# A fused two-layer kernel: second norm and feed-forward in one stage, expert weights in quarters

## The chip, the core and the metric

The kernel runs as one program on one core of a Trainium2 chip. Its time is the device time of one execution in microseconds (us); less is better. The core has five engines that run their own instruction streams and wait for each other through semaphores: PE (matrix products, into the accumulation banks "ps"), DVE (vector operations), ACT (activations and scaled copies), POOL (a second vector engine, slower for the same width) and SP (here only a queue that starts DMA transfers). DMA engines move data and also transpose it.

## The reference

Two layers over x of 4 x 2048 rows of 256 numbers. Each layer is a layer norm, an attention s, a feed-forward g, and x + s * silu(g):

```python
xn = _layernorm(x)
s  = L0_attn(xn)       # linear attention, elu(q)+1, 16 heads
g  = _silu(L0_ffn(xn)) # 16 experts, top 2 by row, and a shared expert
x  = x + s * g
xn = _layernorm(x)
s  = L1_attn(xn)       # retention with decay by head, group norm
g  = _silu(L1_ffn(xn))
return x + s * g
```

The change is mostly about `L1_ffn`. Its two products take operands that are rounded to a 4-bit grid in blocks of 16 numbers, each block scaled by its largest magnitude over 6:

```python
scale = max(max|xb| / 6, 1e-12)
q = grid(|xb / scale|) * sign(xb) * scale  # grid 0 .5 1 1.5 2 3 4 6
gate, y = fp4(x) @ fp4(w_gate).T, fp4(x) @ fp4(w_up).T   # 256 -> 704
g = fp4(silu(gate) * y) @ fp4(w_down).T                  # 704 -> 256
```

## The kernel before

The 8192 rows are 64 tiles of 128 rows. The kernel is a row of stages with a barrier between two; inside a stage each engine walks over the tiles in a software pipeline. `pipeline(eng, count, stages, slots)` is written once per engine with a list of (skew, function): at step c the engine calls, in the order of the list, each function for tile c - skew. So the list is the order of the engine's queue, and an instruction that waits holds up all behind it. The first depth + slots (+ a remainder) steps and the last ones are written out, the rest is a loop with `slots` steps in its body; `unrolled` writes out all.

The stages that matter, with their times in the profiled execution: `phase_dense` (116 to 389 us), `phase_norm_fp4`, named normB (945 to 1097), `phase_ffn` (1097 to 1483), `phase_retention` (1483 to 1838), `phase_output` (1839 to 1909).

normB takes 16 groups of 4 tiles. SP loads a group of x (512 KB, four slots), DVE takes the statistics (`bn_stats`, `bn_aggr`), POOL the reciprocal root, ACT normalises into `xn` and copies the upper part to f16, POOL subtracts for the lower part, and SP turns both (`xT_all`). The rounding is in `Quant`, 1024 wide: on DVE `dve_amax` (L412), `dve_step` (L418), `dve_reciprocal` (L423), `dve_scale` (L432), `dve_round` (L445), `dve_grid` (L451) and `dve_value` (L459), on ACT `act_magic` (L440) and `act_hi` (L464), on POOL `low` (L469). The rounded rows are turned into `xq_T`. PE has nothing to do in this stage.

`phase_ffn` takes one tile a step. PE makes gate and up in two halves of 352 columns (`project(0)`, `project(1)`, 12 products each, lines L197), each in a gate bank and an up bank of its own, and, five tiles later, `down` (L632, 17 products). ACT takes silu of each gate half (`sigmoid`, L647), DVE multiplies it with the up half (`swish`, L674), and the 704-wide result goes through the same `Quant`. SP turns it (`ffn_hT`, four slots), `down` uses it from two banks in turn, and ACT's `output` (L657) writes silu over the tile's place in `xq_T`. PE's `project(k)` waits for `swish(k)` of the tile before, since it writes into the same banks. The weights of the last two stages (`w_pack1`) are loaded and split in f16 parts at the stage's start.

`phase_dense` makes first-layer keys, values, and the shared expert. Meanwhile SP loads one expert's weights every fourth tile (763 columns), ACT makes their upper part (`expert_hi`, L1193), DVE the lower (L1245). `kv_product` (L1131) sums keys x values in one bank over four tiles, then DVE adds that to `kv_sum` (`add_sums`, L1239) and PE waits for it. `phase_retention` is a pipeline with three steps in its loop; DVE's masked product (L2143) comes once a tile. `phase_output` ends with DVE's L2307 and L2311 in groups of four tiles, after POOL's lower parts (L2341).

## Time and profile before

| | |
|---|---|
| median of 3 runs | 1910.14 us (1910.09 to 1916.22) |
| profiled execution | 1911.08 us, its span 1909.3 us |
| mean granted TensorE clock | 0.892 |
| PE busy | 1383.9 us, 72% |
| DVE busy | 1482.7 us, 78% |
| ACT busy | 1183.7 us, 62% |
| POOL busy | 1055.7 us, 55% |
| second norm, PE busy | 0 of 153 us |
| feed-forward, PE busy | 366 of 386 us |

The shares are means over stages with different limits, so no single one tells what bounds the kernel. The stages follow one another with barriers between them, and a stage's length has to be read from the engine that is full in it, or from the loop of waits that closes over it. A granted clock of 1.00 in a stretch is 2.4 GHz.

### The profile page before, as it was taken

The page shows a single profiled execution, that of the slowest core. Times are in us where ns is not written, and L with a number is a line of the kernel's source. Part 1 is how long each engine was busy: PE and PEld are TensorE (multiplying, and loading weights), DVE is VectorE, ACT ScalarE, POOL GpSimd, SP SyncE. Part 2 cuts the span into 40 slices and gives each one's busy share as a digit, 9 for nine tenths or more (in the row PEclk, how much of TensorE's full clock was granted, in tenths as well). Part 3 has the DMA queues.
Part 4 walks back from the last instruction along what each step waited for, and adds up shares of the span by engine and source line. Part 5 has one row for each costly group of instructions (what it writes and reads, how often), then busy time and mean ns, then how long its engine had stood idle before and what let it go on. Part 6 is the DMA issues. An engine that isn't in the chain of part 4 may idle for free. (4 is left out here: it accounts for less than half of the span.)

```text
span 1909.3 us, 63051 instructions
## 1 busy us (share of the span) xinstructions
PE 1383.9 (72%) x21895; PEld 956.3 (50%) x21896; DVE 1482.7 (78%) x3716; ACT 1183.7 (62%) x2966; POOL 1055.7 (55%) x1056
## 2 busy tenths in 40 slices
PE   3469999968998355455300089999998779999957
PEld 3425555546555244344200056666666456666646
DVE  7876777756665599888499789999998568888849
ACT  7637777846666488888266444444444557777746
POOL 6657777733333787775156512222222467777747
PEclk9999999989999677777655599999999999999959
DMA  8636666689997576766469723223223112222229
GB/s 257 194 121 174 188 181 187 179 163 207 213 218 193 164 188 181 189 166 156 134 143 196 146 68 64 65 60 68 60 60 68 41 42 54 51 55 50 55 72 294
DMA packets 487154, 256.17 MB, mean 134 GB/s; under 512 B 357309, under 2 KB 474624, under 8 KB 486528
## 3 DMA queue, kind: packets, MB, share of 16 engines
q1 hardware_dynamic: 474466, 219.10, 46.1%
q0 software_dynamic: 12576, 35.67, 6.4%
q8 instruction: 59, 0.97, 0.2%
q14 instruction: 53, 0.43, 0.1%
HBM read 79.52 MB, written 73.44 MB: 80 GB/s over the span
## 5 line engine op out<-in xcount | busy, mean ns | idle before, releaser
L197 PE MATMUL ps<-all_late,l_xq_T 128*128 128x352 f16 x1536 | 244.4, 317 | 170.1 <-DVEq L185 159.5
L197 PEld LDWEIGHTS ps<-all_late,l_xq_T 128*128 (+1 forms) x1536 | 147.3, 99 | 262.6 <-DVEq L185 160.0
L469 POOL TENSOR_TENSOR ffn_h<-ffn_fq_val,ffn_h 128x704 f16<-128x704 f32 x64 | 97.4, 1522 | 286.9 <-ACT ffn_h L464 286.9
L197 PE MATMUL ps<-l0moe_W,all_xT_all 128*128 128x16 f16 (+2 forms) x1152 | 190.6, 312 | 40.0 <-ACT all_xT_all L828 22.3
L647 ACT ACTIVATE ffn_th<-ps 128x352 f32<-128x352 f32 x128 | 59.3, 463 | 178.3 <-PE ps L197 178.3
L1362 POOL TENSOR_TENSOR all_late<-experts_se,all_mhalf 128x4 f32<-128x4 f32 (+1 forms) x77 | 76.6, 995 | 158.8 <-DVE experts_se L1471 149.6
L2215 POOL TENSOR_TENSOR all_late<-ret_pm,all_late 128x512 f16<-128x512 f32 x128 | 145.5, 1157 | 19.4 <-ACT all_late L2121 19.4
L197 PEld LDWEIGHTS ps<-l0moe_W,all_xT_all 128*128 (+1 forms) x1152 | 83.9, 100 | 122.0 <-ACT all_xT_all L828 26.0
L632 PE MATMUL ps<-all_late,ffn_hT 128*128 128x256 f16 x1088 | 131.7, 276 | 6.0 <-ACT l_xq_T L657 5.4
L197 PE MATMUL ps<-moe_E,experts_gT 128*128 x864 | 117.5, 276 | 16.9 <-DMA experts_gT<-slots_dram 12.4
L1627 PE MATMUL ps<-l_kvm,both_q 128*128 128x136 f16 x384 | 38.9, 272 | 118.4 <-DVE both_o L1800 118.4
L632 PEld LDWEIGHTS ps<-all_late,ffn_hT 128*128 128x128 f16 x1088 | 107.0, 99 | 25.7 <-issue 4.9
L2143 DVE TENSOR_TENSOR ret_pm<-ps,tables_causal 128x1024 f32<-128x1024 f32 x64 | 78.4, 1225 | 44.9 <-PE ps L1988 32.9
L197 PE MATMUL ps<-l1b_W,all_xT_all 128*128 128x512 f16 x384 | 97.1, 392 | 2.4 <-DVEq L1911 2.4
L197 PEld LDWEIGHTS ps<-moe_E,experts_gT 128*128 128x128 f16 x864 | 71.8, 98 | 50.6 <-issue 32.8
L1627 PEld LDWEIGHTS ps<-l_kvm,both_q 128*128 128x128 f16 x384 | 33.2, 121 | 124.2 <-issue 123.9
L2103 ACT ACTIVATE all_late<-ps,tables_parity 128x512 f16<-128x512 f16 x128 | 81.3, 694 | 16.7 <-PE ps L2003 16.7
L1435 ACT ACTIVATE all_late<-ps 128x510 f32<-128x510 f32 x72 | 42.9, 595 | 71.8 <-PE ps L1411 49.5
L2084 ACT ACTIVATE all_xT_all<-ps 128x256 f32 (+1 forms) x64 | 24.5, 383 | 97.1 <-PE ps L2048 97.1
L197 PE MATMUL ps<-moe_E,experts_hT 128*128 x432 | 69.7, 275 | 18.8 <-issue 5.7
L1662 POOL DMA_INDIRECT both_y<-rows_dram,moe_pos_lo x64 | 72.9, 1139 | 18.1 <-issue 16.7
L1615 PE MATMUL ps<-all_xT_all,l_Wq 128*128 128x256 f16 x384 | 67.4, 345 | 20.9 <-DVE both_qp L1781 14.4
(295 smaller groups left out, 4511.1 us busy)
## 6 DMA issues: line engine op xcount, KB each, us to landing
rows_dram<-all_late SPq DMA_DIRECT2D x72, 256.0 KB, 2.5
ret_v<-ret_vpad SPq DMA_DIRECT2D x256, 64.0 KB, 2.0
front_xin<-x SPq DMA_DIRECT2D x16, 512.0 KB, 4.5
x_dram<-front_x SPq DMA_DIRECT2D x16, 512.0 KB, 5.4
all_late<-x_dram SPq DMA_DIRECT2D x64, 128.0 KB, 2.1
z_dram<-all_late SPq DMA_DIRECT2D x64, 128.0 KB
both_zin<-z_dram SPq DMA_DIRECT2D x16, 512.0 KB, 4.8
both_xin<-x SPq DMA_DIRECT2D x16, 512.0 KB, 4.3
```

The costliest lines, as they stand in the source:

```text
L197: mm = pe.matmul(out, lhs[a], rhs[b], start=first and n == 0, stop=last and n == 2, skip_group_check=True)
L469: eng.tensor_tensor(lo, self.shaped(t, hi), hi, ALU.subtract).then_inc(self.lo, 1)
L632: ins = pe.matmul(down_ps[t.slot], hT[:, t.slot4, c % both], DN[:, c], start=c == 0, stop=c == both + FFC - 1, skip_group_check=True)
L647: act.activation(th[:, t.slot, k], gate[k], ACT.Silu, scale=1 / WS).then_inc(s_th[k], 1)
L1362: pool.tensor_tensor(rows[:, n % 4, which, :, 0], se[:, u, which], power[:, which], ALU.pow).then_inc(s_time, 1)
L1435: act.activation(os[t.slot4][:, :, 1:D], op[t.slot], ACT.Copy, scale=1 / WS).then_inc(s_oc, 1)
L1615: ins = pe.matmul(qps[t.slot][:, j], w[a], x[:, :, b * C + c], start=c == 0 and n == 0 and j == 0, stop=c == C - 1 and n == 2, skip_group_ ...
L1627: ins = pe.matmul(nps[:, k, c], q16[:, t.slot, a, c, k * P:(k + 1) * P], kv[b], start=c == 0 and n == 0, stop=n == 2, skip_group_check=True)
L1662: pool.indirect_dma_start(dst[:, slot, k], None, rows_dram, at).then_inc(arrived[slot], 16)
L2103: ins = act.activation(kx16[:, t.slot4].rearrange("p a c s e j -> p (a c s) e j")[:, :, e], src, ACT.Copy, scale=parity[:, e:e + 1])
L2143: dve.tensor_tensor(pm[:, t.slot4], sps, causal[:].unsqueeze(1).to_broadcast([P, 4, RC]), ALU.mult).then_inc(s_p, 1)
L2215: ins = pool.tensor_tensor(p16[:, u, 1, r], pm[:, u, r], p16[:, u, 0, r], ALU.subtract)
```

## The change

**Second norm and feed-forward in one stage.** `phase_norm_ffn` replaces both. Norm and rounding of x go by pairs of tiles (512 wide) on the even or odd steps, eleven steps (K) ahead of the projections of the same tiles. x is loaded by pairs (256 KB) in two slots, and a load waits until ACT has normalised the pair two before. x and xn lie in the memory of the later weights W1, so `w_pack1` is loaded and split at the stage's end.

**Products on POOL.** For the hidden values, `QuantApart` writes the grid to SBUF (`dve_grid`), and the product with the step is POOL's (`pool_value`). The first half of the swish product is POOL's too; it needs the up half in SBUF, so ACT copies it (`up_copy`, 352 wide). `down` has one bank instead of two, its skew is 8 instead of 5, and the turned hidden values have two slots instead of four.

```diff
+def pipeline(eng, count, stages, slots=LAG, head=None):
...
+    start = depth + (slots if head is None else head) + (count - depth) % slots
...
+class QuantApart(Quant):
...
+    def dve_scale(self, dve, t, src):
+        u = t.slot
+        dve.wait_ge(self.rs, done(t))
+        dve.wait_ge(self.q, self.work_free(t))
+        dve.scalar_tensor_tensor(self.b3(self.work[u]), self.b3(src), 1 - 2.0 ** -22,
+                                 self.wide(self.rstep[u]), ALU.mult, ALU.mult).then_inc(self.v, 1)
+    def act_magic(self, act, t):
+        u = t.slot
+        act.wait_ge(self.v, done(t))
+        act.wait_ge(self.xq, free(t))
+        act.activation(self.big[:, u], self.work[u], ACT.Abs, scale=self.MAGIC).then_inc(self.mg, 1)
+    def dve_grid(self, dve, t):
+        u = t.slot
+        dve.wait_ge(self.up, done(t))
+        dve.scalar_tensor_tensor(self.big[:, u], self.big[:, u], self.LEAST, self.work[u],
+                                 ALU.max, ALU.subtract).then_inc(self.q, 1)
...
+    def pool_value(self, pool, t):
+        u = t.slot
+        pool.wait_ge(self.q, done(t))
+        pool.wait_ge(self.hi, free(t))
+        pool.wait_ge(self.lo, free(t))
+        pool.tensor_tensor(self.b3(self.val[:, u]), self.b3(self.big[:, u]), self.wide(self.step[:, u, 0:self.blocks]),
+                           ALU.mult).then_inc(self.xq, 1)
```

```diff
+def phase_norm_ffn(nc, ps, x_dram, mhalf, xT_all, xq_T, GU, DN, W1, apart, loads, jobs):
...
+        h16 = ph.sb("h16", [P, LAG, 2 * FF], F16)
...
+        down_ps = ps[:, 6, 0:D]
+        at = [FF + u * 64 for u in range(2 * LAG)]
+        fq = QuantApart(ph, "fq", FF, 1.0, work=[spare[:, 0:FF]],
+                        rstep=[spare[:, at[u]:at[u] + FF // BLK] for u in range(LAG)])
+        nq = Quant(ph, "nq", U * D, 1.0, work=[ps[:, 7, :]],
+                   rstep=[spare[:, at[LAG + u]:at[LAG + u] + U * D // BLK] for u in range(LAG)])
...
+            def load(p):
+                if p.n >= LAG:
+                    sp.wait_ge(s_xn, p.n - LAG + LAG + 1)
+                sp.dma_start(xin[:, p.slot], x_pairs[p.n]).then_inc(s_xin[p.slot], 16)
...
+            def turn_h(t):
                 sp.wait_ge(fq.lo, done(t))
-                through(sp, s_pass)
...
+                sp.wait_ge(s_down, free(t))
+                sp.dma_start_transpose(hT[:, t.slot], h16[:, t.slot]).then_inc(s_hT[t.slot], 16)
+            unrolled(TILES, [(0, even(load)), (6, even(turn_x)), (9, even(turn_q)), (K + 6, turn_h)], 4)
+            sp.wait_ge(s_wlo, 1)
+            sp.dma_start(stage, jobs[1][0]).then_inc(s_stage[1], 16)
```

```diff
-                    pe.wait_ge(s_h[k], prev(t))
+                    if k == 0:
+                        if t.slot4 % 2 == 0:
+                            pe.wait_ge(s_qturn[t.slot4 // 2], landed(pair_of(t)))
+                        pe.wait_ge(s_th[0], prev(t))
+                        pe.wait_ge(s_upc, prev(t))
+                    else:
+                        pe.wait_ge(s_h[1], prev(t))
...
+                pe.wait_ge(s_g, prev(t))
...
-            pipeline(pe, TILES, [(5, down), (0, project(0)), (0, project(1))], 4)
+            pipeline(pe, TILES, [(8, down), (0, project(0)), (0, project(1))], 4)
...
+                act.wait_ge(nq.v, free(p))
...
+            def up_copy(t):
+                act.wait_ge(s_up[0], done(t))
+                act.activation(up0[:, t.slot], upp[0], ACT.Copy, scale=1 / WS).then_inc(s_upc, 1)
...
-            pipeline(act, TILES, [(0, sigmoid(0)),
-                                  (6, output),
-                                  (0, sigmoid(1)),
-                                  (2, hidden_hi),
-                                  (1, lambda t: fq.act_magic(act, t))], 4)
+                act.activation(out, down_ps, ACT.Silu, scale=1 / WS).then_inc(s_g, 1)
...
+            pipeline(act, TILES, [(K, sigmoid(0)), (K, up_copy), (6, even(lambda p: nq.act_magic(act, p))),
+                                  (K + 5, hidden_hi), (K, sigmoid(1)), (K + 8, output), (3, even(normalise)),
+                                  (4, even(upper)), (7, even(quantised_hi)), (K + 8, weights_hi),
+                                  (K + 2, lambda t: fq.act_magic(act, t))], 4)
```

```diff
+                dve.wait_ge(s_xin[u], landed(Tile(t.n // 2, u, t.n // 4)))
+                dve.bn_stats(stats[:, u, k], xin[:, u, k]).then_inc(s_stats, 1)
...
+                dve.wait_ge(s_th[1], done(t))
+                dve.wait_ge(fq.v, free(t))
+                dve.scalar_tensor_tensor(h[:, u, half:FF], th[:, u, 1], 1 / WS, upp[1],
+                                         ALU.mult, ALU.mult).then_inc(s_h[1], 1)
...
-            pipeline(dve, TILES, [(1, swish(0)),
...
-                                  (2, lambda t: fq.dve_round(dve, t)),
-                                  (1, lambda t: fq.dve_step(dve, t)),
-                                  (2, lambda t: fq.dve_grid(dve, t)),
-                                  (1, lambda t: fq.dve_reciprocal(dve, t)),
-                                  (2, lambda t: fq.dve_value(dve, t)),
-                                  (1, lambda t: fq.dve_scale(dve, t, h[:, t.slot]))])
...
+            pipeline(dve, TILES, [(0, statistics),
+                                  (K + 1, swish),
+                                  (K + 2, maxima),
+                                  (1, even(variance)),
+                                  (K + 3, lambda t: fq.dve_round(dve, t)),
+                                  (K + 2, lambda t: fq.dve_step(dve, t)),
+                                  (5, even(maxima_norm)),
+                                  (6, even(lambda p: nq.dve_round(dve, p))),
+                                  (K + 3, lambda t: fq.dve_grid(dve, t)),
+                                  (K + 2, lambda t: fq.dve_reciprocal(dve, t)),
+                                  (5, even(lambda p: nq.dve_step(dve, p))),
+                                  (6, even(lambda p: nq.dve_grid(dve, p))),
+                                  (5, even(lambda p: nq.dve_reciprocal(dve, p))),
+                                  (5, even(lambda p: nq.dve_scale(dve, p, flat(xn[:, p.slot])))),
+                                  (K + 2, lambda t: fq.dve_scale(dve, t, h[:, t.slot])),
+                                  (6, even(lambda p: nq.dve_value(dve, p))),
+                                  (K + 8, weights_lo)], 4)
...
+                pool.tensor_tensor(h[:, u, 0:half], th[:, u, 0], up0[:, u], ALU.mult).then_inc(s_h[0], 1)
+            pipeline(pool, TILES, [(K + 1, swish),
+                                   (2, even(rsqrt)),
+                                   (K + 4, lambda t: fq.pool_value(pool, t)),
+                                   (5, even(part_lo)),
+                                   (8, even(quantised_lo)),
+                                   (K + 5, lambda t: fq.low(pool, t, h16[:, t.slot, 0:FF], h16[:, t.slot, FF:2 * FF]))], 4)
```

**Dense stage, retention, output.** Expert weights come in quarters (191 columns), one a tile; the key-value sums stay in the bank for a batch of 16 tiles, two banks in turn, and DVE copies them once a batch; PE and DVE are written out. Retention's PE starts its loop three steps earlier. In the output stage `prod` has one buffer.

```diff
+                at = quarter(t.n % 4)
+                sp.dma_start(e_stage[:, t.n % 4, 0:at.stop - at.start], e_dram[t.n // 4][:, at]).then_inc(s_eload[t.n % 4], 16)
             unrolled(TILES, [(7, turn), (0, rows_in), (11, expert_load), (12, store)])
...
+                batch, first = t.n // TB, t.n % TB == 0
+                if first and batch >= 2:
+                    pe.wait_ge(s_kvadd, batch - 1)
...
-                        ins = pe.matmul(sums[:, c, 0:P + 1], keys[x], vals[y], start=c == 0 and n == 0 and t.slot4 == 0,
...
-            pipeline(pe, TILES, [(7, down), (3, kv_product), (0, project)], 4)
+            unrolled(TILES, [(7, down), (3, kv_product), (0, project)], 4)
...
-                if t.slot4 == 0:
-                    act.wait_ge(s_eload, 16 * (t.n // 4) + 16)
...
+                at = quarter(t.slot4)
+                act.wait_ge(s_eload[t.slot4], 16 * (t.n // 4) + 16)
...
+                act.activation(part, e_stage[:, t.slot4, 0:at.stop - at.start], ACT.Copy, scale=WS).then_inc(s_ehi, 1)
+            pipeline(act, TILES, [(8, z_out), (3, hidden_hi), (2, key_hi), (1, nonlinear), (10, expert_hi)], 4)
...
-                dve.tensor_tensor(acc[:, :, 0:P + 1], sums[:, :, 0:P + 1], acc[:, :, 0:P + 1], ALU.add).then_inc(s_kvadd, 1)
+                if t.n % TB == TB - 1:
+                    dve.wait_ge(s_kvs, done(t))
+                    dve.tensor_copy(kv_sum[:, t.n // TB, :, 0:P + 1], sums[t.n // TB % 2][:, :, 0:P + 1]).then_inc(s_kvadd, 1)
...
-                                  (1, elementwise)], 4)
...
+            unrolled(TILES, [(4, add_sums), (3, hidden_lo), (2, key_lo), (1, elementwise), (11, expert_lo)], 4)
...
-            pipeline(pe, TILES, [(4, scores), (3, turn), (0, project), (3, updates), (2, queries), (5, results)], 3)
+            pipeline(pe, TILES, [(4, scores), (3, turn), (0, project), (3, updates), (2, queries), (5, results)], 3, head=0)
...
+                if t.n:
+                    dve.wait_ge(s_sum, t.n)
```

How the order moves: on ACT in the middle of the feed-forward stage, two steps of before (ffn_th is silu of a gate half, l_xq_T the output, ffn_h the upper part, ffn_fq_big the magic number's sum):

```order
L647 ACTIVATE ffn_th<-ps 128x352
L657 ACTIVATE l_xq_T<-ps 128x256
L647 ACTIVATE ffn_th<-ps 128x352
L464 ACTIVATE ffn_h<-ffn_fq_val 128x704
L440 ACTIVATE ffn_fq_big<-ps 128x704
L647 ACTIVATE ffn_th<-ps 128x352
L657 ACTIVATE l_xq_T<-ps 128x256
L647 ACTIVATE ffn_th<-ps 128x352
L464 ACTIVATE ffn_h<-ffn_fq_val 128x704
L440 ACTIVATE ffn_fq_big<-ps 128x704
```

And two steps of after, an even one first (l_apart<-l_W is the pair's upper part, ffn_up the copy of the up half, l_W<-l_W the normalising of a pair, ffn_nq the pair's rounding):

```order
L641 ACTIVATE ffn_th<-ps 128x352
L655 ACTIVATE l_xq_T<-ps 128x256
L631 ACTIVATE l_apart<-l_W 128x2x256
L396 ACTIVATE ffn_fq_big<-ps 128x704
L641 ACTIVATE ffn_th<-ps 128x352
L646 ACTIVATE ffn_up<-ps 128x352
L359 ACTIVATE ffn_h<-ffn_fq_val 128x704
L641 ACTIVATE ffn_th<-ps 128x352
L655 ACTIVATE l_xq_T<-ps 128x256
L624 ACTIVATE l_W<-l_W,ffn_shift,ffn_rstd 128x256 x2
L359 ACTIVATE l_apart<-ffn_nq_val 128x2x256
L396 ACTIVATE ffn_fq_big<-ps 128x704
```

The output now stands behind the second silu of the step instead of ahead of it, and the pair's normalising (x2) behind the output, in every other step.

On DVE, one step of before in the same stage:

```order
L412 TENSOR_REDUCE ffn_fq_amax<-ffn_h 128x44
L445 SCALAR_TENSOR_TENSOR ps<-ffn_fq_big,ps 128x704
L418 TENSOR_SCALAR ffn_fq_step<-ffn_fq_amax 128x45
L451 SCALAR_TENSOR_TENSOR ps<-ffn_fq_big,ps 128x704
L423 RECIPROCAL ps<-ffn_fq_step 128x44
L459 TENSOR_TENSOR ffn_fq_val<-ps,ffn_fq_step 128x704
L432 SCALAR_TENSOR_TENSOR ps<-ffn_h,ps 128x704
L674 SCALAR_TENSOR_TENSOR ffn_h<-ffn_th,ps 128x352 x2
```

And an even step of after (ffn_stats is the norm's statistics of one tile, ffn_nq the pair's rounding):

```order
L676 BN_STATS ffn_stats<-l_W 128x6
L697 SCALAR_TENSOR_TENSOR ffn_h<-ffn_th,ps 128x352
L307 TENSOR_REDUCE ffn_fq_amax<-ffn_h 128x44
L340 SCALAR_TENSOR_TENSOR ps<-ffn_fq_big,ps 128x704
L383 TENSOR_SCALAR ffn_fq_step<-ffn_fq_amax 128x45
L340 SCALAR_TENSOR_TENSOR ps<-ffn_nq_big,ps 128x512
L401 SCALAR_TENSOR_TENSOR ffn_fq_big<-ffn_fq_big,ps 128x704
L318 RECIPROCAL ps<-ffn_fq_step 128x44
L346 SCALAR_TENSOR_TENSOR ps<-ffn_nq_big,ps 128x512
L389 SCALAR_TENSOR_TENSOR ps<-ffn_h,ps 128x704
L354 TENSOR_TENSOR ffn_nq_val<-ps,ffn_nq_step 128x512
```

The statistics, which wait for the load of x, come first in each step, ahead of the one swish half that is left; the value product is gone and three 512-wide operations of the pair are in.

On SP in the middle of the new stage, where before there was one turn of hidden values a tile:

```order
L563 DMA_TRANSPOSE l_xq_T<-l_apart 128x8x128
L576 DMA_TRANSPOSE ffn_hT<-ffn_h 128x11x128
L554 DMA l_W<-x_dram 128x2x256
L558 DMA_TRANSPOSE all_xT_all<-l_apart 128x8x128
L576 DMA_TRANSPOSE ffn_hT<-ffn_h 128x11x128
L563 DMA_TRANSPOSE l_xq_T<-l_apart 128x8x128
L576 DMA_TRANSPOSE ffn_hT<-ffn_h 128x11x128
```

The pair's load (l_W<-x_dram), its two turns, and the turns of hidden values (ffn_hT) share this queue.

## Rows read from the trace of the kernel before

**Rows 1.** The windows by stage: stretch, length, busy time of each engine, PE clock, DMA share.

```profile
944.00:1097.00 153.00, 0.00 (x0) 0.00 (x0) 132.02 (x273) 80.35 (x112) 85.96 (x64) 0.50 0.76 165
1200.00:1460.00 260.00, 255.98 (x1874) 179.96 (x1873) 250.49 (x411) 124.14 (x228) 70.03 (x46) 1.00 0.28 62
1483.00:1556.00 73.00, 54.29 (x1985) 36.02 (x1984) 44.72 (x111) 38.45 (x97) 38.96 (x50) 0.91 0.17 41
650.00:900.00 250.00, 137.30 (x1100) 113.07 (x1101) 220.67 (x546) 206.92 (x503) 192.20 (x155) 0.75 0.68 174
```

**Rows 2.** The line that scales the hidden values: count, min/median/max ns, first and last start.

```profile
L432 DVE SCALAR_TENSOR_TENSOR ps<-ffn_h,ps x64: 895/897/897, 1106.6 to 1468.1; 128x704 f32<-128x704 f32 x64
```

**Rows 3.** The groups of 1103 to 1477 us: busy us, mean ns, idle before, releaser.

```profile
L674 DVE SCALAR_TENSOR_TENSOR ffn_h<-ffn_th,ps 128x352 f32<-128x352 f32 x128 | 60.8, 514 | 6.9 <-ACT ffn_th L647 6.8
L432 DVE SCALAR_TENSOR_TENSOR ps<-ffn_h,ps 128x704 f32<-128x704 f32 x64 | 57.4, 897 | 6.6
L423 DVE RECIPROCAL ps<-ffn_fq_step 128x44 f32<-128x44 f32 x64 | 27.4, 428 | 0.0
L418 DVE TENSOR_SCALAR ffn_fq_step<-ffn_fq_amax 128x45 f32<-128x45 f32 x64 | 11.6, 181 | 0.0
L647 ACT ACTIVATE ffn_th<-ps 128x352 f32<-128x352 f32 x128 | 59.3, 463 | 178.3 <-PE ps L197 178.3
L469 POOL TENSOR_TENSOR ffn_h<-ffn_fq_val,ffn_h 128x704 f16<-128x704 f32 x64 | 97.4, 1522 | 286.9 <-ACT ffn_h L464 286.9
```

**Rows 4.** The groups of 940 to 1103 us (the norm).

```profile
L320 DVE BATCH_NORM_STATS2 normB_stats<-normB_xin 128x6 f32<-128x256 f32 x64 | 22.4, 411 | 2.7 <-DMA normB_xin<-x_dram 2.7
L451 DVE SCALAR_TENSOR_TENSOR ps<-normB_fq_big,ps 128x1024 f32<-128x1024 bf16 x16 | 19.6, 1227 | 0.0
L423 DVE RECIPROCAL ps<-normB_fq_step 128x64 f32<-128x64 f32 x16 | 8.8, 552 | 0.0
L357 ACT ACTIVATE normB_xn<-normB_xin,normB_shift,normB_rstd 128x256 f32<-128x256 f32 x64 | 33.2, 588 | 68.2 <-POOL normB_shift L303 68.2
```

**Rows 5.** The timeline in the feed-forward stage: start, length, instruction, idle before.

```profile
1304.43 3.78 PE L197 MATMUL ps<-all_late,l_xq_T 128*128 128x352 f16 x24
...
1464.03 0.38 ACT L657 ACTIVATE l_xq_T<-ps 128x256 f32<-128x256 f32 x1
1464.55 2.02 PE L632 MATMUL ps<-all_late,ffn_hT 128*128 128x256 f16 x17 [0.73 <-ACT l_xq_T L657]
```

**Rows 6.** The DMA issues: count, KB each, median us from issue to landing.

```profile
all_late<-x_dram SPq DMA_DIRECT2D x64, 128.0 KB, 2.1
normB_xin<-x_dram SPq DMA_DIRECT2D x16, 512.0 KB, 4.4
```

**Rows 7.** Waits of 116 to 389 us: us, times, longest.

```profile
PE ps L1131 <- DVE l0moe_kv_sum L1239: 9.1, 12, 2.8
```

**Rows 8.** PE's timeline in the dense stage, and ACT's at its end.

```profile
144.30 2.75 PE L197 MATMUL ps<-l0moe_W,all_xT_all 128*128 128x512 f16 x12
148.22 2.75 PE L197 MATMUL ps<-l0moe_W,all_xT_all 128*128 128x512 f16 x12
...
215.28 2.75 PE L197 MATMUL ps<-l0moe_W,all_xT_all 128*128 128x512 f16 x12
219.20 2.75 PE L197 MATMUL ps<-l0moe_W,all_xT_all 128*128 128x512 f16 x12
...
386.61 0.84 ACT L1193 ACTIVATE moe_E<-dense_e_stage 128x763 f16<-128x763 f32 x1 [1.65 <-DMA dense_e_stage<-e_pack]
```

**Rows 9.** The masked product's line in two windows: count, first and last start.

```profile
L2143 DVE TENSOR_TENSOR ret_pm<-ps,tables_causal x8: 1224/1225/1226, 1501.8 to 1554.9; 128x1024 f32<-128x1024 f32 x8
...
L2143 DVE TENSOR_TENSOR ret_pm<-ps,tables_causal x25: 1223/1225/1226, 1575.5 to 1695.6; 128x1024 f32<-128x1024 f32 x25
```

**Rows 10.** Waits of 1500 to 1556 us (retention).

```profile
PE ps L1988 <- issue: 8.9, 9, 1.9
```

**Rows 11.** The output stage's low parts on POOL: min/median/max ns.

```profile
L2341 POOL TENSOR_TENSOR out_y<-all_late,out_y x16: 2122/3112/3128, 1850.5 to 1896.3; 128x1024 f16<-128x1024 f32 x16
```

368 lines of the change are left out of this document (163 added, 205 removed).

## The prediction

> **What bounds the kernel now.** I read the windows by stage first, since the page's shares mix stages. In the norm PE does nothing for 153 us, while DVE is busy for 132; in the steady feed-forward PE is busy for 255.98 of 260 us and DVE for 250.49, at a granted clock of 1.00 [rows 1]. So one stage is DVE's alone and the other is nearly full on two engines; the change can give back only idle time of PE in the norm, if DVE has room for the norm. Next, the scaling line gives the pitch of a tile: (1468.1 - 1106.6) / 63 = 5.74 us [rows 2]. A tile then costs PE 5.61 us (255.98 / 260 of 5.7) and DVE 5.49. The norm runs from 944.9 (first load) to 1097.5 and the feed-forward to 1482.8: 537.9 us that the new stage replaces.
>
> **DVE in the new stage.** Per tile before: two swish halves 2 x 0.514, five 704-wide operations (scale, maxima, round, grid, value) at 0.89 by the scale's row, reciprocal 0.428, step 0.181: 6.09 us by sum, 5.49 by the clock, as neighbours overlap (factor 0.90) [rows 1, 3]. The change takes away one swish half and the value product: 6.09 - 0.51 - 0.88 = 4.69, 9.38 a pair. It adds the norm of a pair. A wide operation costs 0.897 at 704 and 1.227 at 1024, so by the line through both 0.70 at 512; five of them 3.46 (maxima and value a little less); two statistics at 0.411; the reciprocal between 0.428 at 44 blocks and 0.552 at 64, by the line 0.35 at 32; five small ones near 0.17 [rows 3, 4]. That is 5.5. Pair: 14.9 by sum, times 0.90 = 13.4 us, 6.7 a tile.
>
> **POOL and ACT.** POOL takes 1.522 us at 704 and, undisturbed, 2.122 at 1024, so 0.86 at 352 and 1.16 at 512 [rows 3, 11]. A pair is 2 x (0.86 + 1.52 + 1.52) + 2 x 1.16 and two small ones for the root, some 11: 5.6 a tile, below DVE. The value product reads a bf16 grid, which no row shows on POOL; between 1.52 and, as in the slow rows of the output stage, 1.52 x 3.112 / 2.122 = 2.2. I take 1.52, because in its own stage the 704-wide operation kept that value beside the same DVE operations; the far end is a rival. ACT gains a 352-wide copy and the pair's work, some 9.6 us a pair, and bounds nothing by its sum.
>
> **The rings.** With sums of 6.7, 5.6 and 5.6, the waits decide. Ring one: `down` now has a single bank, and its output stands behind the second silu on ACT. `down` (tile t) waits for the output of the tile before, which waits for that silu, which waits for the step's last projection. So nothing of PE covers silu 0.46 and output 0.38: 5.61 + 0.1 + 0.46 + 0.38 + 0.14 = 6.65 us a tile. The 0.14 is from the end of output to the next product, 1464.41 to 1464.55; the 0.1 is my value for the way from PE to ACT [rows 3, 5].
>
> Ring two closes over the load, once a pair. A pair's load waits for the normalising of the pair two before, which ACT does behind silu and output in the odd step. The statistics, which wait for the load to land, stand first in DVE's next step, ahead of the swish half for which PE's projection waits. A 256 KB load is between 2.1 (128 KB) and 4.4 us (512 KB) [rows 6]; by the line 2.87. From the odd step's silu: silu 0.44, output 0.36, normalising 2 x 0.588 less overlap 1.08, load 2.87, statistics 0.33, swish 0.51, hand-over 0.15, half of the 24 products (3.78 us [rows 5]) with its run-out 2.01: 7.75. The even half is ring one again, 6.65 with rounding 6.70. 14.45 a pair, 7.23 a tile. It is longer than DVE's 6.7, so DVE waits for the load in each pair. Bounds: with a load of 2.1, 6.84 a tile, with 4.4 it is 7.99. I take 7.23.
>
> **The stage.** Fill until the first projection: 2.9 us for the load and 5.5 pairs at DVE's 4.8 (5.5 x 0.9 less what waits on nothing) = 29. Steps 12 to 18 have no `down`: 7 x 6.6 = 46. Then 45 steps with loads, 45 x 7.23 = 325. Then 11 steps without norm in ring one, 11 x 6.65 = 73. Tail: eight `down` at about 2.5 each through the single bank (1.85 and the output's way), 20, the last weights' split and the barrier 4.5: 24.5. Sum 497.5 against 537.9: **-40.4**. Bounds by the load alone: -57 to -6. One barrier fewer is in this sum.
>
> **Dense stage.** PE waits for the key-value sum 12 times, 9.1 us [rows 7]. The stage is full on PE otherwise (3.92 us a tile both in the written-out head, 144.30 to 148.22, and in the loop, 215.28 to 219.20 [rows 8]), so these 9.1 go. At its end the last output stood behind a weights' part that had waited for a DMA by 1.65 us, until 387.4 [rows 8]; quarters have four slots and land earlier, some 2 us more. ACT and DVE get more instructions for the same columns, in stages where neither is full. **-11**; below it 0 if the waits only move, above it -13.
>
> **Retention.** The masked product comes every (1554.9 - 1501.8) / 7 = 7.6 us in the written-out head and the loop's first pass, and every (1695.6 - 1575.5) / 24 = 5.0 in the loop; and PE idles there on "issue" for 8.9 us in 1500 to 1556 [rows 9, 10]. With three written-out steps fewer, three tiles go at 5.0 instead: 3 x 2.6 = **-7.8**; between 0, if the first pass of the loop costs that much wherever it stands, and -12. The trace says that written-out steps of PE are dearer than the loop. The Trainium skill ("Runtime: NRT & Kernel Launch", section "Instruction fetch mechanics") says that fetching a straight stream is mostly hidden, that taken branches break the prefetch, and that kernels prefer full unrolling where possible. By that rule this edit would bring 0 or lose, and the dense stage's unrolling would be the gain. The trace does not agree in retention, and shows no difference either way in the dense stage.
>
> **Output.** DVE now waits for its own previous sum before L2307. It does L2307 and L2311 in that order anyway, and POOL bounds that stage (most of its operations take 3.1 us [rows 11]): +0.2.
>
> **Sum.** 1911.1 (the profiled execution, 1.0 above the median) - 40.4 - 11 - 7.8 + 0.2 = 1852.1. The forecast is 1852 us, 3.1% less; with the terms' nearer ends 1838 to 1868.
>
> **The rivals.**
> - Load ring does not close. If ACT is far enough ahead of DVE in the odd step, the load is hidden, and DVE with 6.7 bounds the stage: 45 x 0.53 = 24 us less, 1828, from 1815 to 1836. For it speaks that a 128 KB load lands in 2.1 [rows 6]; against it, that ACT's normalising stands behind a silu that waits for PE in the same step.
> - POOL is slowed by DVE. In the output stage POOL's operation goes from 2.122 to a median of 3.112 while DVE adds two operands from SBUF [rows 11]. With a factor 1.47 a pair costs POOL 16.2 us, 8.1 a tile: 52 x 0.87 = 45 more, 1897, from 1875 to 1910. Against it: no wide DVE operation of the new stage has both operands in SBUF, as the old ones had none beside L469, which kept 1.522 [rows 3]. The Trainium skill ("GPSIMD Engine Reference", section "8. Key points") says that POOL shares its SBUF interfaces with DVE and collides with DVE instructions in a two-port mode or with two SBUF inputs. By that rule the output stage slows and this one does not; the trace agrees in both.
> - The smaller parts give nothing. The dense waits were covered by ACT and DVE (DVE waits for ACT there too), and the retention's first loop pass keeps its price: 18.8 us back, 1871.
> - PE's clock falls; this one ends on the other side. PE loses its full share (5.6 of 7.23, 77%) with gaps of 0.9 to 1.3 us in each step. Where it was busy for 137 of 250 us the granted clock was 0.75, and where it was busy for 54 of 73 us, 0.91 [rows 1]. At half speed (1.2 GHz) the 7.7 us of products on ring two double. At a mean of 0.91 (18% of the time at half) a pair costs 1.4 more: +36 us, 1888. At 0.75, 3.85 more: 52 x 1.9 = +100, 1952. The stage has 556.5 us before the whole is no gain; less fill, tail and the last steps that is 8.27 a tile, a mean clock of 0.865. Below this the kernel is slower. For it: the gaps are new. Against it: the gaps are short and evenly spread, and 0.75 was seen at a busy share of 55%.
>
> **How the numbers follow.** Forecast 0.48 (1838 to 1868). Load hidden 0.18. POOL slowed 0.11. Smaller parts nothing 0.08. Clock 0.10, half of it below the deciding 0.865. The remaining 0.05 is spread, mostly upwards. The range for 8 in 10 reaches down over most of the load-hidden case and up over the smaller parts, the milder clock and the lower half of POOL's: 1818 to 1892. About 0.5% (10 us) is what a measurement tells from no change. Faster by more needs less than 1900.6: all of the forecast, the hidden load and the smaller parts, most of POOL and half of the clock: 0.90. Within 0.5%: 0.04. Slower: 0.06, the deep clock and one more in a hundred.
>
> **What would show it.** In the profile after: the scaling line's pitch near 7.2 us with a pair pattern, and DVE's statistics waiting for the load of x by 1 to 2 us a pair (if not, the load is hidden, 6.7). PE idle before `down`, ended by ACT's output, about 1 us a tile. POOL's value product at 1.5 us. The granted clock at 1.00. No PE wait for the key-value sum beyond two, the dense stage 11 us shorter; in retention seven slow masked products instead of ten. It would be wrong if the stage is not between 480 and 530 us long, or if an engine that I left out, SP with its turns and loads in one queue above all, holds the pair.

## The result and the profile after

The changed kernel takes 1917.14 us (median of 11 runs) against 1910.34 us in 11 runs of the kernel before: a ratio of 1.003, with a 95% interval of 1.0017 to 1.0043. Ten of the 11 lie between 1914.55 and 1921.14 us; the eleventh took 2066.71 us at a mean granted clock of 0.724 and is left out of the ratio. That is 0.3% slower, within what I had called no change; forecast was 1852, and the range ended at 1892. The profiled execution takes 1917.14 us, its span 1915.3 (1909.3 before).

First the stages. The dense stage ended at 379.4 instead of 392.1 us. The stage that replaces norm and feed-forward runs from its first load at 933.99 to retention's first product at 1492.1 us: 558.1 us, where the two took 537.9 and I forecast 497.5. So 60.6 of the 65 us that the forecast missed by are in this stage, and what is long in it is DVE's pitch, the time from one tile to the next. The scaling line of the hidden values, as in [rows 2] (count, min/median/max ns, first and last start, of the whole stage and of 1100 to 1296 us):

```profile
L389 DVE SCALAR_TENSOR_TENSOR ps<-ffn_h,ps x64: 874/888/896, 974.2 to 1468.3; 128x704 f32<-128x704 f32 x64
...
L389 DVE SCALAR_TENSOR_TENSOR ps<-ffn_h,ps x24: 874/882/890, 1105.4 to 1294.0; 128x704 f32<-128x704 f32 x24
```

(1294.0 - 1105.4) / 23 is 8.20 us a tile, where I had 7.23, and DVE is full in it (length, then busy us of PE, PEld, DVE, ACT, POOL, and the clock, as in [rows 1]):

```profile
1100.00:1400.00 300.00, 211.60 (x1504) 141.00 (x1503) 275.07 (x490) 150.97 (x311) 193.30 (x182) 1.00 0.45 91
```

DVE is busy for 275 of 300 us, so the profile books 7.5 us of work a tile to it, where I had 6.7. PE is busy for 211.6 at a clock of 1.00. The groups of the stage that answer to [rows 3, 4] (busy us, mean ns, idle before and who ended it):

```profile
L389 DVE SCALAR_TENSOR_TENSOR ps<-ffn_h,ps 128x704 f32<-128x704 f32 x64 | 56.6, 884 | 0.3
L697 DVE SCALAR_TENSOR_TENSOR ffn_h<-ffn_th,ps 128x352 f32<-128x352 f32 x64 | 32.2, 503 | 5.1 <-ACT ffn_th L641 4.5
L307 DVE TENSOR_REDUCE ffn_fq_amax<-ffn_h 128x44 f32<-128x704 f32 x64 | 56.1, 876 | 0.0
L383 DVE TENSOR_SCALAR ffn_fq_step<-ffn_fq_amax 128x45 f32<-128x45 f32 x64 | 55.2, 863 | 32.6 <-POOL ffn_fq_val L409 32.6
L313 DVE TENSOR_SCALAR ffn_nq_step<-ffn_nq_amax 128x33 f32<-128x33 f32 x32 | 5.4, 169 | 0.1
L686 DVE TENSOR_SCALAR ffn_away<-ffn_mv 128x2 f32<-128x2 f32 x32 | 25.3, 790 | 3.0
L687 DVE TENSOR_SCALAR ffn_ve<-ffn_mv 128x2 f32<-128x2 f32 x32 | 9.1, 284 | 0.0
L676 DVE BATCH_NORM_STATS2 ffn_stats<-l_W 128x6 f32<-128x256 f32 x64 | 26.3, 415 | 8.9 <-DMA l_W<-x_dram 8.9
L409 POOL TENSOR_TENSOR ffn_fq_val<-ffn_fq_big,ffn_fq_step 128x704 f32<-128x704 bf16 x64 | 89.5, 1399 | 2.3 <-DVE ffn_fq_big L401 1.8 <-POOL ffn_h L364 0.2
L754 POOL TENSOR_TENSOR ffn_h<-ffn_th,ffn_up 128x352 f32<-128x352 f32 x64 | 59.6, 931 | 164.7 <-DVE ps L389 164.7
L364 POOL TENSOR_TENSOR ffn_h<-ffn_fq_val,ffn_h 128x704 f16<-128x704 f32 x64 | 97.5, 1523 | 15.5 <-ACT ffn_h L359 15.5
```

The wide operations cost what they had cost. But L383, the step of 45 numbers, has gone from 181 to 863 ns, and L686, the sign change of two numbers, takes 790, where before a four-wide one took some 170. Their own line shows the spread:

```profile
L383 DVE TENSOR_SCALAR ffn_fq_step<-ffn_fq_amax x64: 175/1048/1479, 971.9 to 1465.7; 128x45 f32<-128x45 f32 x64
```

175 ns at best, 1479 at worst. What they wait for shows in the timeline (start, length, engine, line; idle before the instruction in brackets):

```profile
1241.25 1.16 POOL L364 TENSOR_TENSOR l_apart<-ffn_nq_val,l_apart 128x512 f16<-128x512 f32 x1
1241.40 1.05 DVE L383 TENSOR_SCALAR ffn_fq_step<-ffn_fq_amax 128x45 f32<-128x45 f32 x1 [1.13 <-POOL ffn_fq_val L409]
...
1247.93 1.15 POOL L743 TENSOR_TENSOR l_apart<-l_W,l_apart 128x512 f16<-128x512 f32 x1
1247.95 1.15 DVE L686 TENSOR_SCALAR ffn_away<-ffn_mv 128x2 f32<-128x2 f32 x1
1249.02 0.16 DVE L687 TENSOR_SCALAR ffn_ve<-ffn_mv 128x2 f32<-128x2 f32 x1
```

At 1241.40 the step starts and lasts until 1242.45; POOL's subtraction ends at 1242.41. At 1247.95 L686 starts and lasts until 1249.10; POOL's ends at 1249.08. The next one, L687, meets POOL between two operations and takes 0.16. So it looks as if a tiny DVE operation is held until POOL's running one is done. All 64 steps agree with that: 57 begin while a POOL operation runs, and each of them ends 0.04 to 0.05 us after it; the seven that begin with POOL idle take 0.18 to 0.19. The rounding of the pair has a step of the same kind, L313, 33 wide. It stays at 169 ns, and 28 of its 32 begin while POOL is idle. In sum 64 x (0.863 - 0.181) = 43.6 us for L383, 32 x 0.62 = 19.8 for L686 and 3.6 for L687: 67 us of busy time that I had not counted. Beside it the step waits for POOL's value product of two tiles before (waits of the whole stage: us, times, longest):

```profile
PE ps L213 <- DVE ffn_h L697: 93.3, 57, 3.8
PE ps L608 <- ACT l_xq_T L655: 57.5, 62, 3.5
DVE ffn_fq_step L383 <- POOL ffn_fq_val L409: 32.6, 33, 1.3
DVE ffn_stats L676 <- DMA l_W<-x_dram: 8.9, 5, 3.5
```

The load's ring, which I had as the bound, costs DVE 8.9 us in all, since DVE comes too late to meet it.

### The profile page after: what moved, and what is told of

Same layout as the page of the kernel before. It is cut to its first block and busy times, and to the rows that moved or that the text cites. A ratio compares the mean times of both kernels' runs of the same rounds, so it can differ in the third digit from the quotient of the medians.

```text
span 1915.3 us, 63179 instructions
## 1 busy us (share of the span) xinstructions
PE 1390.9 (73%) x21895; PEld 953.8 (50%) x21896; DVE 1473.2 (77%) x3767; ACT 1199.0 (63%) x3126; POOL 1205.7 (63%) x1248
## 5 line engine op out<-in xcount | busy, mean ns | idle before, releaser
L213 PE MATMUL ps<-all_late,l_xq_T 128*128 128x352 f16 x1536 | 256.9, 320 | 121.7 <-DVE ffn_h L697 93.3
L396 ACT ACTIVATE ffn_fq_big<-ps 128x704 bf16<-128x704 f32 x64 | 48.5, 757 | 191.3 <-DVE ps L389 191.3
L754 POOL TENSOR_TENSOR ffn_h<-ffn_th,ffn_up 128x352 f32<-128x352 f32 x64 | 59.6, 931 | 164.7 <-DVE ps L389 164.7
L608 PEld LDWEIGHTS ps<-all_late,ffn_hT 128*128 128x128 f16 x1088 | 102.7, 99 | 92.8 <-ACT l_xq_T L655 61.8
L213 PEld LDWEIGHTS ps<-l0moe_W,all_xT_all 128*128 128x128 f16 x1152 | 84.0, 100 | 120.5 <-ACT all_xT_all L889 26.0
L2202 DVE TENSOR_TENSOR ret_pm<-ps,l_apart 128x1024 f32<-128x1024 f32 x64 | 78.4, 1224 | 39.9 <-PE ps L2047 38.5
L213 PE MATMUL ps<-l_W,all_xT_all 128*128 128x512 f16 x384 | 96.7, 389 | 5.9 <-DVEq L1970 4.8
L2162 ACT ACTIVATE all_late<-ps,l_apart 128x512 f16<-128x512 f16 x128 | 81.5, 695 | 18.1 <-PE ps L2062 18.1
L409 POOL TENSOR_TENSOR ffn_fq_val<-ffn_fq_big,ffn_fq_step 128x704 f32<-128x704 bf16 x64 | 89.5, 1399 | 2.3 <-DVE ffn_fq_big L401 1.8
L1494 ACT ACTIVATE all_late<-ps 128x510 f32<-128x510 f32 x72 | 42.9, 596 | 69.0 <-PE ps L1470 36.5
```

Of the source, the lines that this page charges most:

```text
L213: mm = pe.matmul(out, lhs[a], rhs[b], start=first and n == 0, stop=last and n == 2, skip_group_check=True)
L409: pool.tensor_tensor(self.b3(self.val[:, u]), self.b3(self.big[:, u]), self.wide(self.step[:, u, 0:self.blocks]), ALU.mult).then_inc(self. ...
L608: ins = pe.matmul(down_ps, hT[:, t.slot, c % both], DN[:, c], start=c == 0, stop=c == both + FFC - 1, skip_group_check=True)
L754: pool.tensor_tensor(h[:, u, 0:half], th[:, u, 0], up0[:, u], ALU.mult).then_inc(s_h[0], 1)
L2162: ins = act.activation(kx16[:, t.slot4].rearrange("p a c s e j -> p (a c s) e j")[:, :, e], src, ACT.Copy, scale=parity[:, e:e + 1])
L2202: dve.tensor_tensor(pm[:, t.slot4], sps, causal[:].unsqueeze(1).to_broadcast([P, 4, RC]), ALU.mult).then_inc(s_p, 1)
```

## The experiments

The theory (A): DVE's small tensor_scalar has SBUF on both sides and needs an access to SBUF that it shares with POOL; it can't start its work while a POOL operation runs. The rival (B): nothing is held, the long operations are waits for POOL's value or for a result, booked as busy time. Ratios are against the kernel before, run beside them on the same chip. The chips differ a little (the kernel before took 1915.92 us beside some of these runs and 1911.85 beside others), so runs are compared by their ratios or by the length of the stage, which is that of the profiled execution.

**One operand from a bank.** The step takes its floor of 1e-12 from an accumulation bank, so the operation is another kind with the same work. The pair's step (L313) is changed in the same way.

```diff
-        dve.tensor_scalar(self.step[:, u], self.amax[:, u], 1 / 6, 1e-12, ALU.mult, ALU.max).then_inc(self.st, 1)
+        dve.scalar_tensor_tensor(self.step[:, u], self.amax[:, u], 1 / 6, self.floor, ALU.mult, ALU.max).then_inc(self.st, 1)
```

> The changed kernel, but DVE's step operation takes its second operand from an accumulation bank (scalar_tensor_tensor with a constant 1e-12 there) in place of the immediate; same width, place and result. Theory A (the small tensor_scalar with SBUF on both sides is held until the POOL operation that runs ends): the step's mean falls from 863 ns to about 200, the stage from 558 us to about 525, the time to about 1884 us; the norm's away operation stays at about 790 ns. Rival B (the 863 ns are a wait for POOL's value product, or for a result, that is booked as busy time): the mean stays over 700 ns and the time at 1917.

Measured: 1879.51 us, ratio 0.980 (0.978 to 0.982), stage 520.0 us. Of the profile's groups, the step and L686, still of the old kind (here L696):

```profile
L388 DVE SCALAR_TENSOR_TENSOR ffn_fq_step<-ffn_fq_amax,ps 128x45 f32<-128x45 f32 x64 | 12.6, 197 | 32.7 <-POOL ffn_fq_val L414 32.7
L696 DVE TENSOR_SCALAR ffn_away<-ffn_mv 128x2 f32<-128x2 f32 x32 | 25.3, 789 | 3.0
```

The step is at 197 ns and the sign change, which was left alone, at 789. The pair's step, which had not been slow, went from 169 to 174 ns, so it has no part in the gain. B is wrong: the wait for POOL's value is still there, as idle time of 32.7 us beside the operation, as it was before the edit.

**The variance's two operations as well.** They also move behind `dve_round` in DVE's list.

```diff
-                dve.tensor_scalar(away[:, p.slot], mv[:, p.slot, :, 0], -1.0, None, ALU.mult)
-                dve.tensor_scalar(ve[:, p.slot], mv[:, p.slot, :, 1], EPS_LN, None, ALU.add).then_inc(s_ve, 1)
+                dve.scalar_tensor_tensor(away[:, p.slot], mv[:, p.slot, :, 0], -1.0, spare[:, 1008:1010], ALU.mult, ALU.add)
+                dve.scalar_tensor_tensor(ve[:, p.slot], mv[:, p.slot, :, 1], 1.0, spare[:, 1010:1012], ALU.mult, ALU.add).then_inc(s_ve, 1)
...
-                                  (1, even(variance)),
                                   (K + 3, lambda t: fq.dve_round(dve, t)),
+                                  (1, even(variance)),
```

> As the run before, and the norm's two small operations away and ve take a second operand from a bank too, and stand behind the round operation. Theory A: away falls from 790 ns to about 180, 32 x 0.6 = 20 us of DVE, the time to about 1866. Rival B: no change from the run before.

Measured: 1864.34 us, ratio 0.973 (0.971 to 0.974). The stage is 496.7 us long. My sum for it was 497.5. The profiled execution was the fastest of the four, though (1857.37 us): by the medians this edit brought 15.2 us, and the 23.3 by which the stage is shorter than in the run before are too many.

```profile
L696 DVE SCALAR_TENSOR_TENSOR ffn_away<-ffn_mv,ps 128x2 f32<-128x2 f32 x32 | 5.0, 156 | 2.9
L686 DVE BATCH_NORM_STATS2 ffn_stats<-l_W 128x6 f32<-128x256 f32 x64 | 26.7, 421 | 24.4 <-DMA l_W<-x_dram 24.4
```

L696 is at 156 ns, and DVE's idle time before the statistics, ended by the load, has risen from 8.9 to 24.4 us: the load's ring comes into sight as DVE gets faster.

**The same by itself.** A stage behind the output, in the changed kernel, in which DVE does six of each of eight kinds, twice over, in one execution; POOL's subtractions begin at 1926.7 us, when the first round has done the 45- and 2-wide kinds, and fill the whole second.

```diff
+                pool.tensor_tensor(pc[:, n % 4], a[:], b[:], ALU.subtract)   # x72, from SBUF, 704 wide
...
+                    dve.tensor_scalar(o[:, part, n, 0, 0:45], x[:], 1 / 6, 1e-12, ALU.mult, ALU.max)
+                    dve.scalar_tensor_tensor(o[:, part, n, 1, 0:45], x[:], 1 / 6, pz[:, 0:45], ALU.mult, ALU.max)
+                    dve.tensor_scalar(o[:, part, n, 2, 0:45], pz[:, 0:45], 1 / 6, 1e-12, ALU.mult, ALU.max)
+                    dve.tensor_scalar(po[:, 48 * n:48 * n + 45], x[:], 1 / 6, 1e-12, ALU.mult, ALU.max)
+                    dve.tensor_tensor(o[:, part, n, 3, 0:45], x[:], y[:], ALU.max)
+                    dve.tensor_scalar(o[:, part, n, 4, 0:2], x[:, 0:4:2], -1.0, None, ALU.mult)
+                    dve.scalar_tensor_tensor(w[:, part, n, 0:352], a[:, 0:352], 1.0, pz[:, 0:352], ALU.mult, ALU.mult)
+                    dve.tensor_reduce(o[:, part, n, 5, 0:44], c[:], AX, ALU.max)   # by 16
```

> The changed kernel with a stage of its own at the end, in which DVE runs eight kinds of operation six times each, first with POOL idle, then beside POOL's back-to-back 704-wide subtractions from SBUF (1.52 us each). Theory A: the tensor_scalar with SBUF at both ends (45 wide and 2 wide) and the tensor_tensor with two SBUF operands take about 0.18 us alone and up to 1.5 us beside POOL; with one operand or the result in a bank, 0.2 in both; the 352-wide product with one bank operand and the 704-wide maxima do not change. Rival B: none of them changes, or all by the same factor.

The groups of that stage (busy us of all 12, mean ns):

```profile
L2421 POOL TENSOR_TENSOR probe_pc<-probe_a,probe_b 128x704 f32<-128x704 f32 x72 | 117.0, 1667 | 17.3 <-DVEq L2432 17.3
L2443 DVE TENSOR_TENSOR probe_o<-probe_x,probe_y 128x45 f32<-128x45 f32 x12 | 10.3, 925 | 0.0
L2435 DVE TENSOR_SCALAR probe_o<-probe_x 128x45 f32<-128x45 f32 x12 | 9.9, 894 | 0.0
L2445 DVE TENSOR_SCALAR probe_o<-probe_x 128x2 f32<-128x2 f32 x12 | 5.5, 534 | 0.0
L2449 DVE TENSOR_REDUCE probe_o<-probe_c 128x44 f32<-128x704 f32 x12 | 9.7, 882 | 0.0
L2447 DVE SCALAR_TENSOR_TENSOR probe_w<-probe_a,ps 128x352 f32<-128x352 f32 x12 | 5.3, 515 | 0.0
L2439 DVE TENSOR_SCALAR probe_o<-ps 128x45 f32<-128x45 f32 x12 | 1.5, 193 | 0.0
L2437 DVE SCALAR_TENSOR_TENSOR probe_o<-probe_x,ps 128x45 f32<-128x45 f32 x12 | 1.5, 192 | 0.0
L2441 DVE TENSOR_SCALAR ps<-probe_x 128x45 f32<-128x45 f32 x12 | 1.5, 195 | 0.0
```

and DVE's timeline, first two kinds before POOL begins, then the second round, six of a kind in a row:

```profile
1922.79 0.65 DVE L2435 TENSOR_SCALAR probe_o<-probe_x 128x45 f32<-128x45 f32 x6
1925.32 0.78 DVE L2443 TENSOR_TENSOR probe_o<-probe_x,probe_y 128x45 f32<-128x45 f32 x6
...
1933.77 9.23 DVE L2435 TENSOR_SCALAR probe_o<-probe_x 128x45 f32<-128x45 f32 x6
1942.92 0.74 DVE L2437 SCALAR_TENSOR_TENSOR probe_o<-probe_x,ps 128x45 f32<-128x45 f32 x6
1943.59 0.75 DVE L2439 TENSOR_SCALAR probe_o<-ps 128x45 f32<-128x45 f32 x6
1944.26 0.72 DVE L2441 TENSOR_SCALAR ps<-probe_x 128x45 f32<-128x45 f32 x6
1944.90 9.49 DVE L2443 TENSOR_TENSOR probe_o<-probe_x,probe_y 128x45 f32<-128x45 f32 x6
1954.32 4.98 DVE L2445 TENSOR_SCALAR probe_o<-probe_x 128x2 f32<-128x2 f32 x6
```

A was right in each kind. Six tensor_scalars with SBUF at both ends take 0.65 us alone and 9.23 beside POOL, about one for each POOL operation (1.67 us); with the operand or the result in a bank it is 0.72 to 0.75 for six. Two SBUF operands (L2443) go from 0.78 for six to 9.49. The 704-wide maxima from SBUF to SBUF take 882 ns beside POOL, and took 0.89 us in the kernel before: width and place alone don't decide, the kind does. The two tensor_scalars with a bank at one end (L2439, L2441) are of the slow kind and stay fast, so the first edit's gain comes from the bank and not from the other operation. POOL's 72 operations all take 1660 to 1673 ns and begin 1.62 to 1.63 us apart, with DVE at work or not: the short DVE operations cost POOL nothing, and only DVE pays.

**The wait for POOL's value.** Four slots for the step values.

```diff
-        dve.wait_ge(self.xq, free(t))
-        dve.scalar_tensor_tensor(self.step[:, u], ...)
+        dve.scalar_tensor_tensor(self.step4[:, t.slot4], ...)
```

> As the run before, and the step values have four slots, so that DVE's step operation does not wait for POOL's value product two tiles before. If that wait (32.6 us of DVE idle in the changed kernel) is on the path: another 10 to 30 us less, about 1845 us. If it is only where DVE happens to wait for POOL, the wait moves to the round operation and the time stays within 5 us.

Measured: 1857.91 us, ratio 0.969 (0.966 to 0.971), and a stage of 495.1 instead of 496.7. The time fell by 6.4 us by the medians. That is less than the 10 to 30 of a wait on the path; the second expectation, 5 at most, holds nearly, but DVE's idle time moved to the load (36.5 us) and not to the round operation:

```profile
L690 DVE BATCH_NORM_STATS2 ffn_stats<-l_W 128x6 f32<-128x256 f32 x64 | 26.7, 422 | 36.5 <-DMA l_W<-x_dram 36.5
```

and its waits of 1050 to 1350 us (us, times, longest):

```profile
PE ps L618 <- ACT l_xq_T L665: 35.9, 43, 0.9
DVE ffn_stats L690 <- DMA l_W<-x_dram: 21.2, 20, 2.0
```

These are the two rings of the prediction, and (1296.2 - 1099.7) / 28 = 7.02 us a tile is close to its 7.23. Whether they bind, the next two tell, each made alone on top of the four slots.

**Ring one: ACT's output first in its step.**

```diff
-            pipeline(act, TILES, [(K, sigmoid(0)), (K, up_copy), ..., (K, sigmoid(1)), (K + 8, output), (3, even(normalise)),
+            pipeline(act, TILES, [(K + 8, output), (K, sigmoid(0)), (K, up_copy), ..., (K, sigmoid(1)), (3, even(normalise)),
```

> The kernel with four step slots (1858 us), and ACT's output stands first in its step, ahead of the first silu, so the single bank of the down product is read before PE has finished the step's projections. Its tile pitch is 7.02 us in 1100 to 1296 us. If ring one is on the path (PE waits for the output 43 times, 35.9 us in 1050 to 1350): those waits go, the pitch falls towards DVE's 6.4 to 6.6, the time by about 18 to about 1840. If the load's ring alone sets the pair (DVE then waits longer for the load): the time falls by 5 or less.

Measured: 1830.40 us, ratio 0.958 (0.956 to 0.959), stage 472.0 us.

**Ring two: DVE's statistics and variance late.**

```diff
-            pipeline(dve, TILES, [(0, statistics),
+            pipeline(dve, TILES, [
...
-                                  (1, even(variance)),
...
+                                  (0, statistics),
+                                  (1, even(variance)),
                                   (K + 2, lambda t: fq.dve_scale(dve, t, h[:, t.slot])),
```

> The kernel with four step slots, and DVE takes the statistics and variance of the norm near the end of its step instead of at its start, so that the load has most of a step to land. If the load's ring is on the path (36.5 us of DVE idle for the load in the whole stage): the idle time goes, the pitch falls to ring one's 6.65, about 17 us less, 1841. If it is only slack of a DVE that waits anyway: no change, and DVE's idle time moves to the swish half.

Measured: 1830.03 us, ratio 0.958 (0.956 to 0.960), stage 472.1 us. Both stages are 23 us shorter than with four slots alone, and the ratio falls from 0.969 to 0.958 (some 22 us), where I expected 17 or 18; both come to the same place. The pitch in 1100 to 1296 us, of the one and of the other:

```profile
L397 DVE SCALAR_TENSOR_TENSOR ps<-ffn_h,ps x29: 878/882/889, 1104.6 to 1292.5; 128x704 f32<-128x704 f32 x29
```

```profile
L397 DVE SCALAR_TENSOR_TENSOR ps<-ffn_h,ps x29: 876/892/894, 1105.4 to 1292.2; 128x704 f32<-128x704 f32 x29
```

187.9 / 28 and 186.8 / 28: 6.71 and 6.67 us a tile, which is DVE's own sum of the prediction, 6.7. With four slots alone the scaling line begins by turns 7.38 and some 6.65 us after the one before. With the output first it is 7.38 and some 6.05: the load still holds one half of the pair (DVE waits 20.6 us for it in the stage, 36.5 before the edit), and DVE makes up for it in the other. So it takes both rings, one in each half, to exceed DVE's pair. The two runs don't part ring one from DVE cleanly: with the statistics late PE still waits for the output in each tile (24.1 us in 29 times in this window), and 6.67 is ring one's own 6.65 as well.

**All of it, and the output stage.** DVE's product there goes back into the bank, so the addition behind it has one operand from SBUF.

```diff
-                dve.scalar_tensor_tensor(prod[:], ops[t.n % TURNED], 1 / WS, g1_all[...], ALU.mult, ALU.mult).then_inc(s_prod, 1)
+                dve.scalar_tensor_tensor(ops[t.n % TURNED], ops[t.n % TURNED], 1 / WS, g1_all[...], ALU.mult, ALU.mult).then_inc(s_prod, 1)
...
-                dve.tensor_tensor(x1[:, u], prod[:], x1[:, u], ALU.add).then_inc(s_sum, 1)
+                dve.tensor_tensor(x1[:, u], ops[t.n % TURNED], x1[:, u], ALU.add).then_inc(s_sum, 1)
```

> Output first and statistics late together, and in the output stage DVE writes its product back into the accumulation bank, so that its addition has one operand from SBUF instead of two. In the norm and feed-forward stage DVE is left as the bound at about 6.4 us a tile: 28 us less. In the output stage, if the held SBUF access is what makes POOL's operation 3.1 us long instead of 2.1: POOL at 2.1 us, 16 x 0.95 = 15 us less. Together about 1815 us. If POOL's 3.1 us have another cause, the output stage stays and the time is about 1830.

Measured: 1823.56 us, ratio 0.953 (0.951 to 0.955): the best version, 4.7% faster than the kernel before, and faster than the changed one by more. The edit has a third part: PE writes into that bank only after the addition, not after the product. In the same window as above, both rings off give no shorter pitch than one (6.74 us), since DVE is full, with 188.09 of 196 us:

```profile
1100.00:1296.00 196.00, 163.68 (x1198) 114.62 (x1197) 188.09 (x393) 118.47 (x247) 154.97 (x146) 1.00 0.55 111
```

The stage is 467.4 us long, 4.6 less than with either edit alone. Against the late statistics alone that is gained in its last steps, where no norm is left for DVE: from the 51st tile's scaling line to the last they come every 5.34 us, and every 5.85 with the statistics late alone. There ring one does bind by itself.

In the output stage the two lines (busy us, mean ns):

```profile
L2418 POOL TENSOR_TENSOR out_y<-all_late,out_y 128x1024 f16<-128x1024 f32 x16 | 34.2, 2137 | 11.9 <-ACT out_y L2405 11.9
L2388 DVE TENSOR_TENSOR out_x<-ps,out_x 128x1024 f32<-128x1024 f32 x16 | 19.6, 1225 | 1.4 <-DMA out_x<-x_dram 0.9
```

POOL is at a mean of 2137 ns, where it had 2830 in the run with the output first (and a median of 3112 before [rows 11]), and DVE's addition at 1225 instead of a mean of 1630 in the changed kernel. So the cause of the 3.1 us is shown. But from its first product to the end the output stage takes 53.5 us, where it took 56.6 in the run with the output first: 3 us less, not 15. With the full 15 the time would be near the 1815 us that I expected. POOL is busy for 11 us less (34.2 instead of 44.9), and its idle time that ACT's copy ends went from 6.8 to 11.9 us; that ACT bounds the stage next is a guess, which no run tries.

**The small parts alone**, on the kernel before, with the old norm and feed-forward stages (the edits are those shown above for the dense stage, `head=0` and `prod`).

> The kernel before with the dense stage's edit, the retention's shorter head and the single buffer of the output stage, but with the old norm and feed-forward stages. My prediction's terms: -11 and -7.8 and +0.2, 1892 us. By the stages of the changed kernel's trace: dense -12.7, retention -5.5, about 1893. Rival: the three give nothing, 1910.

Measured: 1897.49 us, ratio 0.990 (0.988 to 0.992), 1.0% less, 18.4 us by the medians (by the interval 15 to 24), and 18.6 was the sum. The key-value wait is gone from PE's waits, and retention's masked products:

```profile
L2155 DVE TENSOR_TENSOR ret_pm<-ps,tables_causal x64: 1224/1225/1226, 1484.6 to 1816.5; 128x1024 f32<-128x1024 f32 x64
```

run over 331.9 us instead of 338.9 (the same line before: 1491.7 to 1830.6). Not all of these 7.0 us reach the end: from its first product to the output stage's first operation retention takes 353.2 us, and 356.3 before.

## Why the prediction was wrong

**DVE in the new stage: the step that failed.** The prediction priced DVE's small operations as if a running POOL could not touch them. So DVE came to 6.7 us a tile and the load's ring, with 7.23, was the bound; measured were 7.5 us of DVE a tile at a pitch of 8.20, and DVE was the bound. The step of "reciprocal 0.428, step 0.181" was taken at its duration in a stage in which POOL was busy for 70 of 260 us, and the two of the variance, among the "five small ones near 0.17", at theirs in the old norm, where all 16 of each begin with POOL idle. POOL is busy for 193 of 300 us in the new stage, and a small tensor_scalar beside it costs what is left of POOL's operation. The term was 0.18 for L383 and measured 0.863, 0.17 for L686 and measured 0.790; in sum 67 us of DVE. Replacing the two kinds took 38.1 and then 23.3 us off the stage in the profiled executions (the second 15.2 off the medians). With them the forecast's stage of 497.5 is there, at 496.7, but that it fits so well is luck. In that run the first projection comes after 21.5 us (29 in the sum), the first `down` after 52.9 more (46), the last projection's end after 391.1 more (325 + 73), and then it takes 31.2 to the end (24.5): four errors of some 7 us each that cancel.

**The rule was weighed against the wrong operations.** For the rival "POOL is slowed by DVE" I checked the wide operations and asked only what POOL loses. The small ones were the ones that collide, and DVE lost. I had the rule before me: the Trainium skill ("GPSIMD Engine Reference", section "8. Key points") says that POOL shares its SBUF interfaces with DVE, and collides with DVE instructions in a two-port mode or with two SBUF inputs. The runs agree for two SBUF inputs (0.78 us alone for six, 9.49 beside POOL); the mode of a tensor_scalar no run shows, only that it is held. My "the trace agrees in both" could not be right for the new stage, of which there was no trace. The Trainium skill ("SBUF — State Buffer", section "SBUF: two separate sides") goes further: the shared pair is held for a whole instruction and the other engine blocks fully. The runs agree: 9.23 us for six tensor_scalars that take 0.65 us alone. The trace of before had a hint that I passed over. The norm's step had a mean of 311 ns there, against 181 in the feed-forward stage:

```profile
L418 DVE TENSOR_SCALAR normB_fq_step<-normB_fq_amax 128x65 f32<-128x65 f32 x16 | 5.0, 311 | 0.0
```

Fifteen of these 16 took 186 to 198 ns and one took 2129, as long as the norm's wide POOL operations (2.1 us).

**POOL.** The value product from a bf16 grid took 1.399 us (1.52 assumed), the 352-wide swish half 0.931 (0.86). The rival "POOL slowed by DVE" was wrong for POOL and right in its pair of engines.

**The rings.** Right in mechanism, and hidden behind DVE in the changed kernel. In the run with four step slots PE waits for the output in every tile and DVE for the load in nearly every pair, at 7.02 against 7.23: the half of the pair behind the load takes 7.38 us, where the sum had 7.75. (The terms written for ring one add up to 6.69, not to 6.65; the other half takes some 6.65.) What I had not seen is that while the norm runs the two rings only bind together: take either away and DVE's 6.7 shows.

**Fill and tail.** The first projection came 21.5 us after the first load (29 forecast), the last part 35 us after the last projection (24.5): the last two tiles' steps on DVE are held again, for 1.4 and 1.5 us, and the second weights' load stands behind the last turn.

**The rest.** Dense: -12.7 against -11. Retention was sized too high: the stretch of its masked products is 5.5 us shorter in the changed kernel and 7.0 alone, but the whole stage only 4.1 and 3.1, against -7.8. With the new stage (+20.2), the stages between dense and norm, which the change leaves alone (+1.8), and the output stage (+0.9, against +0.2) that makes 6.1, and the spans differ by 6.0.

**The clock** stayed at 1.00 in the stage with PE busy for 71% of it; gaps of 0.8 to 1.7 us did not cost it. I had given 0.04 to a time within 0.5% of the old one and 0.06 to a slower one; what brought the kernel there is none of the mechanisms behind these chances.

## What to carry to other kernels

When work is put on POOL, list DVE's operations by kind, the smallest too. Here a tensor_scalar from SBUF to SBUF, and in the stage by itself a tensor_tensor with two SBUF operands, paid the rest of the POOL operation that ran, and an operand or the result in an accumulation bank took it out of the way for some 0.01 us (0.192 to 0.195 instead of 0.180). A short operation whose maximum is near the duration of another engine's operations is suspected of a wait, whatever the busy column says; whether it begins beside one of these and ends with it tells.
